# Routing shares moved forward, both halves of z scaled early in the choosing pairs, and all eight experts computed by tiles

## What is computed

```
x = x + _L0_attn_ref(_layernorm(x, axis=-1), L0_attn_w_q, L0_attn_w_k, L0_attn_w_v, L0_attn_w_o)
x = x + _L0_ffn_ref(_layernorm(x, axis=-1), L0_ffn_Wr, L0_ffn_W1, L0_ffn_W2)
# attention: returns h + z with z = (softmax(q k^T / 8) v) w_o, h its normalised input; q, k, v = h w_q, h w_k, h w_v
# experts, t = 4096 tokens of 128, E = 8, F = 512, cap = t / E = 512:
probs = softmax(xf @ Wr); eidx = argmax(probs); p_tok = probs[eidx]
rank = number of earlier tokens with the same eidx; keep = rank < cap
xe = xf[dispatch]                          # up to 512 tokens of each expert
h = maximum(einsum("ecd,edf->ecf", xe, W1), 0)
ye = einsum("ecf,efd->ecd", h, W2) * p_tok[dispatch]
y[dispatch] += ye; returns xf + y
```

## Time and profile before

| | |
|---|---|
| time of the three runs | 1517.62, 1520.93, 1526.56 us |
| the profiled execution | 1521.67 us, of which 1519.5 us is the span of the trace |
| TensorE matmuls | 1484.4 us busy, 98% of the span; mean granted clock 0.988 |
| GpSimd | 1220.3 us, 80% |
| VectorE | 998.1 us, 66% |
| ScalarE | 794.0 us, 52% |
| first expert's first layer starts | 1451.00 us |

### The profile page before, as it was taken

One profiled execution on the slowest core, in us unless ns is written; L12 is line 12 of the kernel. 1 busy time (PEld: TensorE's weight loads), 2 busy tenths in 40 slices (PEclk: granted clock), 3 DMA queues, 4 the chain that ended last, 5 costly groups with the idle time before them and its releaser, 6 DMA issues.

```text
span 1519.5 us, 21578 instructions
## 1 busy us (share of the span) xinstructions
PE 1484.4 (98%) x7180; PEld 842.8 (55%) x7180; DVE 998.1 (66%) x1236; ACT 794.0 (52%) x1556; POOL 1220.3 (80%) x679
## 2 busy tenths in 40 slices
PE   8999999999999999999999999999999999999996
PEld 5455555555555555555555555555555555545585
DVE  6557667776767656676676656676776666675553
ACT  4565546555565555565545554555555555544351
POOL 5888779899798877898788878899789889887545
PEclk9999999999999999999999999999999999998998
DMA  5334444442344443442343444432344443340421
GB/s 145 86 84 94 93 112 112 101 107 67 74 103 93 105 99 89 100 90 53 89 105 89 109 93 96 99 77 69 87 92 105 110 99 68 76 99 10 136 79 33
DMA packets 125294, 137.88 MB, mean 91 GB/s; under 512 B 44107, under 2 KB 69198, under 8 KB 125185
## 3 DMA queue, kind: packets, MB, share of 16 engines
q1 hardware_dynamic: 118784, 130.26, 36.9%
q0 software_dynamic: 2048, 4.10, 0.8%
q10 hardware_dynamic: 4352, 2.13, 0.5%
HBM read 16.81 MB, written 8.45 MB: 17 GB/s over the span
## 4 chain that ended last, share of the span: by engine, by line
PE 89%; DVE 4%; POOL 2%; issue 1%; ACT 1%; SPq 1%; DMA 1%; another core or an unknown queue 0%; POOLq 0%; ACTq 0%; DVEq 0%
PE ps_w L1455 28%; PE ps_w L1439 16%; PE ps_w L1440 14%; PE ps_m L1387 10%; PE ps_m L1488 4%; POOL acc L695 2%; PE ps_w L1473 2%; PE ps_m L1355 2%; PE ps_m L1356 2%; PE ps_m L1357 2%; DVE mxw L1112 1%; PE ps_m L1372 1%; PE ps_m L1373 1%; PE ps_m L1374 1%; DVE z L1126 1%
## 5 line engine op out<-in xcount | busy, mean ns | idle before, releaser
L695 POOL TENSOR_TENSOR acc<-acc,ring 128x1024 f32<-128x1024 f32 x382 | 918.9, 2406 | 55.2 <-ACT ring L869 7.8
L1112 DVE TENSOR_REDUCE mxw<-ps_m 128x1 f32<-128x1024 f32 x512 | 601.6, 1217 | 333.6 <-PE ps_m L1387 324.4
L869 ACT ACTIVATE ring<-ps_w 128x512 f32<-128x512 f32 x1024 | 545.4, 600 | 256.8 <-PE ps_w L1440 234.6
L1455 PE MATMUL ps_w<-ring,V 128*64 128x512 f32 x2048 | 469.0, 600 | 0.0
L1439 PE MATMUL ps_w<-queriesA,keysA 128*128 128x512 f32 x1024 | 434.2, 424 | 4.2 <-ACT sums L860 1.5
L1440 PE MATMUL ps_w<-queriesB,keysB 65*128 65x512 f32 x1024 | 408.7, 399 | 0.0
L1455 PEld LDWEIGHTS ps_w<-ring,V 128*64 128x64 f32 x2048 | 136.0, 137 | 266.8 <-issue 238.3
L695 POOL TENSOR_TENSOR acc<-ring 128x1024 f32<-128x1024 f32 x64 | 152.0, 2376 | 163.5 <-PE ps_w L1473 155.4
L1439 PEld LDWEIGHTS ps_w<-queriesA,keysA 128*128 128x128 f32 x1024 | 195.2, 191 | 105.4 <-issue 49.5
L1440 PEld LDWEIGHTS ps_w<-queriesB,keysB 65*128 65x128 f32 x1024 | 195.9, 191 | 34.1 <-issue 0.7
L1387 PE MATMUL ps_m<-keysA,queriesA 64*128 64x512 f32 x1000 | 183.5, 445 | 2.6 <-issue 1.9
(11 more groups left out here) (202 smaller groups left out, 995.2 us busy)
## 6 DMA issues: line engine op xcount, KB each, us to landing
queriesA<-qk_high SPq DMA_DIRECT2D x248, 128.0 KB
keysB<-qk_high SPq DMA_DIRECT2D x124, 128.0 KB
keysA<-qk_rest SPq DMA_DIRECT2D x124, 128.0 KB
queriesB<-qk_rest SPq DMA_DIRECT2D x124, 128.0 KB
by_sums<-sums SPq DMA_DIRECT2D x240, 64.0 KB
keysA<-qk_high SPq DMA_DIRECT2D x93, 128.0 KB
tokens_by_slot<-blank ACTq DMA_DIRECT2D x16, 130.0 KB, 3.2
ring<-tokens_by_slot SPq DMA_DIRECT2D x8, 260.0 KB, 4.7
```

Of the source, the lines that this page charges most:

```text
L695: pool.tensor_tensor(acc[h][:, :], before, P_both(kt), ALU.add).then_inc(summed, 1)
L869: act.activation(P_tile(kt, p), ps_s[k % 3][:, :], ACT.Exp, scale=SCALE).then_inc(exp_done, 1)
L1112: dve.tensor_reduce(mxw[h][:, p * HT + qt:p * HT + qt + 1], ps_m[p][:, :], AX_X, ALU.max).then_inc(maxed, 1)
L1455: mm = pe.matmul(ps_z[p * DK:(p + 1) * DK, :], V_of(j, kt, p), P_tile(kt, p), start=(kt == 0), stop=(kt == KT - 1))
```

## The change

- In the choosing pairs 24, 26 and 28 and in pair 30 (`both`), VectorE scales both halves of z in quarter 1, no half in quarter 3, and takes the fourth reciprocal in quarter 2, right behind the third, not in quarter 3. In the other pairs these stay where they were, but stand behind `choose`, `find_slots` and `find_shares` in the code, so that in pairs 25, 27 and 29 the slots come ahead of the scaling.
- `find_shares` stands right behind `find_slots`, ahead of the row maxima of that quarter and not behind them.
- All eight experts are computed by tiles, with three banks for the first layer. The split of w2, the copies and the turning back are gone; the rectified first layer has two buffers of its own.

```diff
@@ -93,12 +93,7 @@

             xeT_high, xeT_low = ([sb_later(f"{n}{i}", [P, HALF], F32R) for i in range(2)]
                                  for n in ("xeT_high", "xeT_low"))
-            w2_high, w2_low = (sb_later(n, [P, FC * E * D], F32R) for n in ("w2_high", "w2_low"))
-
-            rT = sb_later("rT", [P, FC * HALF], F32R)
-            rT_low = sb_later("rT_low", [P, FC * HALF], F32R)
-            rT_last = w1_sb[:, 0:FC * HALF]
-            yT = sb_later("yT", [P, HALF])
+            rT = [sb_later(f"rT{i}", [P, FC * HALF]) for i in range(2)]
             ye = [sb_later(f"ye{i}", [P, HALF]) for i in range(2)]
...
@@ -285,33 +273,12 @@
         centre_bank = [ps_s[0], ps_s[1], ps_s[2], ps_z]
-        WHOLE = E - 4
-        up_banks = [*ps_s, lent_out]
-
-        def up_no(n):
-            return n % 4 if n < WHOLE * FC else (n - WHOLE * FC) % 3
-
         def up_bank(n):
-            return up_banks[up_no(n)]
-        def chunk_ahead(n):
-            return max((k for k in range(n) if up_no(k) == up_no(n)), default=None)
-
...
+            return ps_s[n % 3]
+        def down_bank(st):
             return [ps_z, lent_out][st % 2][:, 0:P]
-
-        def chunk(a, c):
-            return a[:, c * HALF:(c + 1) * HALF]
-
-        def w2_of(a, e):
-            return a[:, :].rearrange("p (c e d) -> p c e d", c=FC, e=E)[:, :, e, :]

         def qk_bank(j, use):
             return {(1, 0): ps_s[2], (1, 2): lent_turn}.get((j, use), lent_qk)
...
@@ -956,35 +918,15 @@
                     act.wait_ge(up_done, FC * (e - 1))
                 act.activation(xeT_high[e % 2][:, :], ps_t[e % 2], ACT.Copy).then_inc(xeT_split, 1)

-            def high_relu(e, c):
-                act.wait_ge(up_done, e * FC + c + 1)
-                act.activation(chunk(rT, c), up_bank(e * FC + c), ACT.Relu).then_inc(relu_high, 1)
-
...
-            act.wait_ge(w2_loaded, 16 * FC)
-            for e in range(WHOLE):
-                act.activation(w2_of(w2_high, e), w2_of(w2_sb, e), ACT.Copy).then_inc(w2_high_split, 1)
-
             ps_t = [lent_qk, lent_turn]
             high_tokens(0)
-            for e in range(WHOLE):
-                for c in range(FC):
-                    if e > 0 and c == 0:
-                        act.wait_ge(relu_low, FC * e)
-                    high_relu(e, c)
-                high_tokens(e + 1)
-                copy_down(e)
-            for e in range(WHOLE, E):
-                if e > WHOLE:
-                    act.wait_ge(last_down, ST * (e - WHOLE))
+            for e in range(E):
+                if e >= 2:
+                    act.wait_ge(down_done, ST * (e - 1))
                 for c in range(1, FC, 2):
                     act.wait_ge(up_done, e * FC + c + 1)
-                    act.activation(chunk(rT_last, c), up_bank(e * FC + c), ACT.Relu).then_inc(relu_done[1], 1)
+                    act.activation(rT[e % 2][:, c * HALF:(c + 1) * HALF], up_bank(e * FC + c),
+                                   ACT.Relu).then_inc(relu_done[1], 1)
                 if e + 1 < E:
                     high_tokens(e + 1)

@@ -1212,16 +1154,21 @@
                         recip(j - 1, 1, 1)
                     if oct == 3 and known(j, LAST - 1):
                         recip(j, 0, 1)
-
-                    if oct in (0, 2) and j >= 2 and not last:
-                        scale_z(j - 2, oct // 2)
-                    if oct == 2 and not first and not last:
-                        recip(j - 1, 1, 3)
                     if routed(j, "c") is not None and oct == 2:
                         choose(routed(j, "c"), lent_turn)
                         shift(routed(j, "c"))
                     if routed(j, "d") is not None and oct == 0:
                         find_slots(routed(j, "d"), lent_turn)
+                        find_shares(routed(j, "d"))
+
+                    both = routed(j, "c") is not None or known(j, LAST - 1)
+                    if j >= 2 and not last:
+                        if oct == 0 or oct == 2 and not both:
+                            scale_z(j - 2, oct // 2)
+                        if oct == 0 and both:
+                            scale_z(j - 2, 1)
+                    if oct == 2 and not (first or last or both):
+                        recip(j - 1, 1, 3)
                     if not (last and oct >= 1):
                         if oct in (1, 3) and not (first and oct == 1):
                             dve.wait_ge(c_turned, 2 * j + (1 if oct == 1 else 2))
@@ -1234,7 +1181,7 @@
                         scale_z(j - 1, 0)
                     if oct == 1 and not first:
                         recip(j - 1, 1, 2)
-                    if oct == 1 and last:
+                    if oct == 1 and not first and (last or both):
                         recip(j - 1, 1, 3)
                     if oct == 3 and known(j, LAST - 1):
                         recip(j, 0, 2)
@@ -1245,8 +1192,6 @@
                         second_moments(routed(j, "a"), oct // 2)
                     if routed(j, "c") is not None and oct == 2:
                         add_totals(routed(j, "c"))
-                    if routed(j, "d") is not None and oct == 0:
-                        find_shares(routed(j, "d"))
                     if known(j, 2) and oct == 1:
                         dve.tensor_scalar(centre[:, :], ident[:, :], -1.0 / D, None, ALU.add).then_inc(centre_ready, 1)

...
@@ -1305,22 +1242,13 @@
                 dve.tensor_tensor(w1_low[:, piece], centre_bank[e % 4], w1_high[:, piece].bitcast(F32),
                                   ALU.subtract).then_inc(w1_ready, 1)
             low_tokens(0)
-            for e in range(WHOLE):
-                for c in range(FC):
-                    low_relu(e, c)
-                low_tokens(e + 1)
-                if e > 0:
-                    finish(e - 1, range(ST))
-            dve.wait_ge(down_done, WHOLE)
-            for e in range(WHOLE, E):
-                if e > WHOLE:
-                    dve.wait_ge(last_down, ST * (e - WHOLE))
+            for e in range(E):
+                if e >= 2:
+                    dve.wait_ge(down_done, ST * (e - 1))
                 for c in range(0, FC, 2):
                     dve.wait_ge(up_done, e * FC + c + 1)
-                    dve.tensor_scalar(chunk(rT_last, c), up_bank(e * FC + c), 0.0, None,
+                    dve.tensor_scalar(rT[e % 2][:, c * HALF:(c + 1) * HALF], up_bank(e * FC + c), 0.0, None,
                                       ALU.max).then_inc(relu_done[0], 1)
-                if e == WHOLE:
-                    finish(e - 1, range(ST))
                 finish(e, [0])
                 if e + 1 < E:
                     low_tokens(e + 1)
@@ -1751,68 +1679,36 @@
                     mm = pe.transpose(ps_t[e % 2][:, i * P:(i + 1) * P], xe(e)[:, i, 0:D], ident[:, :])
                 mm.then_inc(xe_turned, 1)

-            def up(e):
-                pe.wait_ge(xeT_ready, e + 1)
-                for c in range(FC):
-                    n = e * FC + c
-                    had = chunk_ahead(n)
-                    if had is not None and had < WHOLE * FC:
-                        pe.wait_ge(relu_low, had + 1)
-                    elif had is not None:
-                        pe.wait_ge(relu_done[had % 2], (had - WHOLE * FC) // 2 + 1)
-                    w = slice(e * F + c * P, e * F + (c + 1) * P)
-                    pe.matmul(up_bank(n), w1_low[:, w], xeT_high[e % 2][:, :], start=True, stop=False)
-                    pe.matmul(up_bank(n), w1_high[:, w], xeT_low[e % 2][:, :], start=False, stop=False)
-                    pe.matmul(up_bank(n), w1_high[:, w], xeT_high[e % 2][:, :], start=False, stop=True).then_inc(up_done, 1)
-
             def down(e):
-                w_high, w_low = (w2_of(a, e) for a in (w2_high, w2_low))
...
-            def turn_outputs(e):
-                pe.wait_ge(down_copied, e + 1)
-                if e > 0:
-                    pe.wait_ge(ye_ready, ST * e)
-                for i in range(ST):
-                    mm = pe.transpose(down_bank(e, i), yT[:, i * P:(i + 1) * P], ident[:, :])
-                mm.then_inc(y_turned, 1)
-
-            def last_tiles(e):
                 for st in range(ST):
-                    if st >= 2:
-                        pe.wait_ge(ye_ready, e * ST + st - 1)
+                    n = e * ST + st
+                    if n >= 2:
+                        pe.wait_ge(ye_ready, n - 1)
                     for c in range(FC):
                         if st == 0:
-                            pe.wait_ge(relu_done[c % 2], FC // 2 * (e - WHOLE) + c // 2 + 1)
-                        mm = pe.matmul(down_bank(e, st), rT_last[:, c * HALF + st * P:c * HALF + (st + 1) * P],
+                            pe.wait_ge(relu_done[c % 2], FC // 2 * e + c // 2 + 1)
+                        mm = pe.matmul(down_bank(st),
+                                       rT[e % 2][:, c * HALF + st * P:c * HALF + (st + 1) * P],
```

(21 more changed lines are left out.)

44 lines of the change are left out of this document (2 added, 42 removed).

## The result

The changed kernel takes 1511.48 us in the median of eight runs (1507.69 to 1515.65), the kernel before in eight runs beside it 1520.87: ratio 0.9941 (new over old), 95% interval [0.9923, 0.9958], 9.0 us less (0.0059 x 1520.87). The forecast was 1507.0 with a range of 1501 to 1514.5: the sign is right and the time lies in the range, 4.5 us above the forecast. Of the 14.7 us that the sum promised, 9.0 came.

The account below looks back on a forecast made before the run. The prediction took TensorE's own pace, busy 98% of the span, to bound the kernel; 1.9 + 2.7 + 4.9 + 5.2 = 14.7 us off the profiled 1521.7 gave 1507.0 us, with a range of 1501 to 1514.5.

Parts of the forecast that it names:

- Visits, 1.9 us: Pairs 24 to 29: five TensorE waits vanish as choose and find_slots come ahead of scalings; 1.9 us, bounds 0 and 2.2.
- the next cause that I had as the bound: Visits of pairs 24 to 29: gain 0 if another cause of waiting is right behind the removed one.
- Pair 29, 2.7 us: Pair 29: stall for row maxima behind a held shares instruction goes, with its slow clock; 2.7 of 3.3 us counted.
- Pair 30, 4.9 us: Pair 30, quarter 4: earlier reciprocal and spread remove the copied-sums stall and slow clock behind it; 4.9 us, bounds 1.5 and 5.
- pair 31's stall: VectorE's scaling and reciprocals at pair 30's end: late next, as now; left unchanged, no gain counted.
- quarter 1 of the choosing pairs: Second scaling there delays the maxima, covered by the product with the values: cost 0, bound 0.7 us in each of four pairs.
- Experts, 5.2 us: Experts 4 and 5: one tile form for all eight removes the gap at the change of form; 5.2 us, bounds -1.8 and 5.3.
- rival (a): Experts' gap isn't tied to the change of form and returns at its present size: 1514.3 us, chance 0.14.
- (b): Pair 30: the copy of the sums waits for another thing, so the stall stays: 1511.9 us, chance 0.08.
- (d): Experts: three banks and VectorE's order hand lateness from expert to expert, 3.7 us each: 1536 us, chance 0.04.
- Rival (c): Pair 31's stall goes too, with the slow clock behind it, another 4.9 us: 1502.1 us, chance 0.10.

Follow-up runs that it names:

- the three moved scalings: Changed kernel with pair 29's two scalings and pair 30's first moved to where GpSimd issues no additions: 1504.67 us, ratio 0.9907 against the kernel before.
- the repeat on chip 15: The changed kernel, unchanged, run again beside the kernel before on another chip: 1511.95 us against 1520.2, ratio 0.9955.
- the third experiment: Kernel before with scaling and fourth reciprocal moved behind the routing for all pairs, shares ahead of them: 1514.12 us, ratio 1.0034.
- its two parts: Kernel before with only the experts changed, 1511.42 us, ratio 1.0018; with only attention and routing changed, 1508.83 us, ratio 1.0000.

## Why the prediction was right, and where not

**Visits, 1.9 us: right but for one.** Each choosing pair's quarter 3 fell from 11.8 to 11.5, pair 25's quarter 1 by 0.5. The visit of pair 29 still idles 0.5 us in the first profile and in that of the three moved scalings, and not in the repeat on chip 15: in the first profile `find_slots` waits 0.59 us for the ranks there, which is the next cause that I had as the bound. The cause named, an instruction in front of `choose` or `find_slots`, was it; the third experiment shows that where the scaling goes decides the sign.

**Pair 29, 2.7 us: mechanism right, size off.** The profiled pair gave all 3.3 us. But of the seven traces with the old order of the shares' instruction only two have that stall (three have a smaller one in pair 27, 0.3 to 0.5 us), of the seven with the new order none. As a mean that is 3.3 us times its frequency, 0.9, which is 1.8 us less than I counted.

**Pair 30, 4.9 us: the stall was right, its price and what follows it were not.** Quarter 4 takes 10.0 (forecast 9.9), the spread starts 5.2 us earlier (5.4). But the 14.8 us of that quarter in the kernel before were the longest of seven. All seven traces with the old pair 30 have the same wait there, 1.5 us; the quarter takes 11.7 us in three, 13.3 in three and 14.8 in one, as the granted clock stays at 1.00 or falls to 0.87 or 0.77 on the mean of the quarter. Two of them (only the experts changed, chip 8; kernel before, chip 15):

```profile
1364.49:1376.17 11.68, 10.17 (x51) 5.35 (x49) 8.93 (x8) 5.49 (x11) 10.81 (x5) 1.00 0.09 23
...
1363.82:1377.11 13.29, 11.76 (x52) 6.68 (x50) 8.93 (x9) 5.60 (x11) 12.28 (x6) 0.87 0.08 21
```

So this step gave 2.8 us on the mean and not 4.9: that the clock falls behind this stall was read from one execution and isn't the rule.

The failed step is "What is late next is VectorE's row of scaling and reciprocals at the end of the quarter, as it is now; that is pair 31's stall, which I leave". I held that stall constant. In the traces with the old pair 30 the wait at pair 31's output projection is 0.5 to 2.1 us, and quarter 1 takes 11.5 to 17.7 us; with the new one it is 1.0 us, and quarter 1 takes 12.0. But pair 31's copy of the sums waits for two scalings in a row. With pair 30 ending earlier both fall on an addition each, and quarter 2 takes 13.2 us in place of 8.7 to 9.3, in each of the four traces with pair 30 changed and those scalings in place (14.5 in one). From the start of pair 30 to the first expert the seven traces with the old pair 30 take 112.9 to 117.3 us, 115.0 on the mean; three with the whole change of the attention 113.9 to 114.2: a net gain of 0.9 in place of 4.9. With the three scalings moved it is 109.5, which shows where the rest was.

I had the rule for it: the Trainium skill, SBUF — State Buffer, section "SBUF: two separate sides", says that of GpSimd and a VectorE instruction with two inputs in SBUF whichever starts first keeps the ports for its whole instruction. By it, the second of two scalings in a row may be held like the first; I priced this for quarter 1 of the choosing pairs, where it cost nothing, and not in pair 31. The second scaling's record agrees: its addition had started 0.34 us earlier. The first's doesn't: it starts 0.27 us ahead of the addition (0.24 to 0.28 in all four traces) and is held all the same. What the traces show without doubt is the hold, and not whose start decides.

**Experts, 5.2 us: right, on the chips that show the gap.** The profile gave 4.2 (48.78 for a forecast of 47.7); the third tile's 0.2 us, in five of the seven experts, is the difference, and it is absent on chip 8 (6.76 an expert, in all 47.4 us against 46.4 in the old form; there the first tile is scaled 0.04 to 0.11 us behind its last matmul). That the gap is tied to the change of form was right only through what it does to GpSimd: removing one expert's stores with the form unchanged takes it away, and a long row of stores without a change of form brings it back. So rival (a) was right that the gap isn't tied to the form as such and wrong that it would return: neither trace of the changed kernel has it. Rivals (b) and (d) didn't occur. Rival (c), that pair 31's stall goes too, came out reversed: pair 31 takes 40.7 us, and 38.5 on the mean before.

**What the sum lacked.** By the means of the traces: pairs 24 to 29 -2.2 (268.1 to 265.9), from pair 30 to the first expert -0.9, experts about -4.7 where the kernel before has the gap: 7.8 us, and 9.0 and 6.8 (0.0045 x 1520.2, chip 15) were measured. Single traces also differ by a slow quarter 3 of pair 24 or 28, 3 us at a clock of 0.77 without a stall, in five of fourteen, of old and new kernels alike. The profile after had none and was 3.2 us below its kernel's median.

**Left open.** The kernel before has no trace on chip 8. Its 1508.4 us is what the mildest forms seen elsewhere add up to (1064.4 + 266.2 + 112.9 + 46.4 + 15.8 = 1505.7 us of span, with some 2 us around it), so there pair 31 may take back all that pair 30 gives. No trace shows whether that is so. The whole change wasn't run there; its two parts at 1.0018 and 1.0000 say no gain.
